# Three of four blocks of cross-attention exponentials and maxima moved one place ahead in a software pipeline of four engines

## The reference

```python
# cross-attention, 8 heads of 64, no mask
xn  = layernorm(x)
sim = einsum('bihd,bjhd->bhij', xn @ Wq, ctx @ Wk) / 8
x   = x + (softmax(sim) @ (ctx @ Wv)) @ Wo + bo
# attention whose projections are mixtures of 16 experts
h   = layernorm(x)
rw  = gating(h)                       # softmax over the active experts, [tokens, 16]
q, k, v = [einsum('bte,bted->btd', rw, einsum('btc,ecd->bted', h, w)) for w in (q_proj, k_proj, v_proj)]
attn  = softmax(causal(q @ k.T / 8)) @ v
mixed = attn[:, :, None, :] * rw[..., None]
x   = x + einsum('bted,edc->btc', mixed, o_proj)
```

## Time and profile before

| what | us |
|---|---|
| time, median of 3 runs | 2771.4 (2769.01 to 2772.56) |
| profiled execution, its own time | 2767.65 |
| its span, from the first to the last instruction | 2765.9 |
| TensorE busy (matmuls) | 2698.9 |
| VectorE busy | 2233.7 |
| ScalarE busy | 1226.8 |
| GpSimd busy | 1186.2 |

### The profile page before, as it was taken

One profiled execution on the slowest core, in us unless ns is written; L12 is line 12 of the kernel. 1 busy time (PEld: TensorE's weight loads), 2 busy tenths in 40 slices (PEclk: granted clock), 3 DMA queues, 4 the chain that ended last, 5 costly groups with the idle time before them and its releaser, 6 DMA issues.

```text
span 2765.9 us, 65910 instructions
## 1 busy us (share of the span) xinstructions
PE 2698.9 (98%) x19012; PEld 2582.4 (93%) x19012; DVE 2233.7 (81%) x6371; ACT 1226.8 (44%) x4240; POOL 1186.2 (43%) x1739
## 2 busy tenths in 40 slices
PE   5999999999999999999999999999999999999996
PEld 4999999999999999999999999999999999999996
DVE  6788888888888888888888878888888888888875
ACT  4444444444444444544444444444445444444441
POOL 1353443444444444534434434444445344344343
PEclk8999999999999999999999999999999999999998
DMA  4111111111111111111111111211111111111111
GB/s 105 29 46 43 33 44 35 41 44 28 44 48 28 44 44 32 44 44 32 44 39 37 44 28 44 48 28 44 45 32 44 44 32 44 42 34 44 33 39 39
DMA packets 131437, 113.59 MB, mean 41 GB/s; under 512 B 24720, under 2 KB 130640, under 8 KB 131408
## 3 DMA queue, kind: packets, MB, share of 16 engines
q1 hardware_dynamic: 131408, 113.23, 16.9%
HBM read 95.38 MB, written 17.83 MB: 41 GB/s over the span
## 4 chain that ended last, share of the span: by engine, by line
PE 90%; ACT 4%; DVE 2%; issue 2%; POOL 0%; DMA 0%; DVEq 0%; ACTq 0%; SPq 0%; POOLq 0%
PE bank_b L373 12%; PE bank_b L374 11%; PE bank_b L375 11%; PE bank_a L375 10%; PE bank_a L374 10%; PE bank_a L373 10%; PE bank_c L373 5%; PE bank_c L375 5%; PE bank_c L374 5%; PE bank_a L487 4%; PE bank_c L551 1%; PE bank_a L447 1%; PE bank_a L446 1%; PE bank_a L418 1%; DVE k_stack L1011 1%
## 5 line engine op out<-in xcount | busy, mean ns | idle before, releaser
L373 PE MATMUL bank_b<-wqkv_hi,x2T_lo 128*128 128x384 f32 (+1 forms) x2048 | 719.8, 351 | 0.0
L374 PE MATMUL bank_b<-wqkv_lo,x2T_hi 128*128 128x384 f32 (+1 forms) x2048 | 693.8, 339 | 0.0
L375 PE MATMUL bank_b<-wqkv_hi,x2T_hi 128*128 128x384 f32 (+1 forms) x2048 | 688.7, 336 | 0.0
L1000 DVE SCALAR_TENSOR_TENSOR acc<-bank_b,rw,acc 128x192 f32<-128x192 f32 x1792 | 641.1, 406 | 4.9 <-PE bank_b L375 2.4
L1256 POOL TENSOR_TENSOR mixs_lo<-mix,mixs_hi 128x512 fp32r<-128x512 f32 x256 | 380.5, 1517 | 156.4 <-ACT mixs_hi L777 156.4
L373 PEld LDWEIGHTS bank_b<-wqkv_hi,x2T_lo 128*128 128x128 f32 x2048 | 386.1, 189 | 17.6 <-DVE acc L1000 17.2
L374 PEld LDWEIGHTS bank_b<-wqkv_lo,x2T_hi 128*128 128x128 f32 x2048 | 386.2, 189 | 0.0
L375 PEld LDWEIGHTS bank_b<-wqkv_hi,x2T_hi 128*128 128x128 f32 x2048 | 385.2, 188 | 0.0
L1178 POOL TENSOR_TENSOR pow_out<-pow_in,expo 128x2 f32<-128x2 f32 (+1 forms) x128 | 111.7, 873 | 607.6 <-DVE pow_in L862 508.3
L723 ACT ACTIVATE probs<-bank_a,s_max 128x77 f32<-128x77 f32 x1024 | 316.5, 330 | 56.6 <-DVE s_max L931 56.6
L373 PE MATMUL bank_c<-wo_hi,mixs_lo 128*128 128x256 f32 x1024 | 293.8, 287 | 3.7 <-POOL mixs_lo L1256 3.7
(11 more groups left out here) (195 smaller groups left out, 6926.9 us busy)
## 6 DMA issues: line engine op xcount, KB each, us to landing
rw_all<-rw_dram SPq DMA_DIRECT2D x128, 512.0 KB, 5.9
xt<-in_x_dram SPq DMA_DIRECT2D x64, 256.0 KB, 2.7
out_dram<-mix SPq DMA_DIRECT2D x64, 256.0 KB, 2.2
ct<-in_ctx_dram SPq DMA_DIRECT2D x64, 57.8 KB
ct<-in_ctx_dram SPq DMA_DIRECT2D x64, 19.2 KB
mix<-in_L_ffn_o_proj_dram SPq DMA_DIRECT2D x2, 512.0 KB, 4.4
rw_dram<-rwT SPq DMA_DIRECT2D x64, 16.0 KB, 1.4
x_tiles<-in_L_xattn_Wq_dram SPq DMA_DIRECT2D x1, 512.0 KB, 6.8
```

The lines of the kernel that those rows point to most:

```text
L373: nc.tensor.matmul(dst, lhs[1], rhs[0], start=start, stop=False)
L374: nc.tensor.matmul(dst, lhs[0], rhs[1], start=False, stop=False)
L375: return nc.tensor.matmul(dst, lhs[0], rhs[0], start=False, stop=stop)
L1000: V.scalar_tensor_tensor(acc[:, t, k, :], src, rw[:, t, e:e + 1], acc[:, t, k, :], ALU.mult, ALU.add).then_inc(b_evac, 1)
```

## The change

On VectorE the maxima of blocks 1, 2 and 3 of batch i+1 move from the start of step i+1 to the end of step i: block 1 behind c_pT and ahead of b_qkv 0, block 2 behind b_qkv 0, block 3 behind c_mix 0. On ScalarE the exponentials of blocks 1, 2 and 3 move in the same way: block 1 ahead of the copy of the attention result (c_pv), block 2 behind it, block 3 behind the rounding c_mix 0. No instruction is added or removed; the lists of TensorE, GpSimd and SyncE stay as they are.

```diff
 # ScalarE
                 do(earlier, c_mix, 3)
-                do(now, a_exp, 1)
-                do(now, a_exp, 2)
-                do(now, a_exp, 3)
                 do(now, a_pT, 0)
...
                 do(ahead, a_exp, 0)
+                do(ahead, a_exp, 1)
                 do(before, c_pv)
+                do(ahead, a_exp, 2)
                 do(before, c_mix, 0)
+                do(ahead, a_exp, 3)
                 do(before, c_mix, 1)
                 do(before, c_mix, 2)
 # VectorE
-                do(now, a_s, 1)
                 do(before, b_qkv, 5)
                 do(now, a_psum, 0)
-                do(now, a_s, 2)
-                do(now, a_s, 3)
                 do(before, b_qkv, 6)
                 do(now, a_psum, 1)
...
                 do(ahead, a_s, 0)
                 do(now, b_wsum)
                 do(before, c_pT)
+                do(ahead, a_s, 1)
                 do(now, b_qkv, 0)
+                do(ahead, a_s, 2)
                 do(now, b_qkv, 1)
                 do(now, b_qkv, 2)
                 do(before, c_mix, 0)
+                do(ahead, a_s, 3)
                 do(before, c_mix, 1)
```

## The result

The changed kernel takes 2824.7 us in the median of 4 runs (2822.9 to 2826.1), the kernel before 2770.8 beside it: a ratio of 1.0194, 95% interval 1.0176 to 1.0212, 54 us slower. The forecast was 2827.

The account below looks back on a forecast made before the run. TensorE, 98% busy, bounds the kernel, and VectorE's chain to b_qkv 4 delays it one for one. Three maxima (1.17 us) less 0.26 give 0.91 us, times 62 is 56 us: 2827 as the median, range 2799 to 2850.

Parts of the forecast that it names:

- a delay of 0.91 us in each of 62 steps: VectorE's b_qkv 4: 1.17 us of added maxima less 0.26 us given back; 62 times 0.91 is 56 us.
- VectorE's chain: VectorE's unbroken work from the first block's maximum to b_qkv 4, which TensorE's b_qkv 7 awaits; three maxima add 1.17 us.
- the wait for L1000: TensorE's wait for VectorE's accumulation: to grow from 17.2 to some 70 us, on two products instead of one.
- The starts worked out for the new order: VectorE's computed times: mixing 0 at 1038.79, mixing 1 at 1039.78, mixing 2 at 1041.03, b_qkv 4 at 1042.10.
- The term given back: Mixing 2 on VectorE stands 0.26 us less, as GpSimd's first remainder starts later beside it.
- the hold goes both ways: VectorE's multiply and GpSimd's remainder block each other: delay 0.91 us; 0.78 if only VectorE were held up.
- ScalarE hides the copy: Attention result's copy, delayed some 0.8 us, ends near 1038.3, before mixing 0 at 1038.79: 0.5 us to spare.
- The feared tie at the first rounding: ScalarE's third exponentials end as mixing 0's rounding is due, 1039.50; held back over 0.8 us, 2799 would follow (10%).
- The wait at b_qkv 6: TensorE waits some 0.35 us for b_qkv 3, ending 1.17 us later on VectorE; contained in b_qkv 7's wait.
- The waits of VectorE for the exponentials: Waits at L937 at the step's start, 0.98 us in the step shown: to go, with nothing gained on TensorE.
- The first steps: Steps at the kernel's start: same work in the same order on ScalarE, counted at nothing.
- rival (b): Same delay of 0.1 to 0.5 us, remainder still first: 1.2 to 1.6 us a step, 2846 to 2870; 9%.

Follow-up runs that it names:

- the maxima alone: Changed kernel with the exponentials of blocks 1 to 3 back at the start of the next step, maxima left moved: 2824.7 us, ratio 1.0192.
- one maximum at the head: Kernel before with only block 1's maximum moved ahead of b_qkv 0 on VectorE: 2792.0 us, ratio 1.0078.
- mixing from PSUM: Changed kernel with mixing multiplies reading the attention result from PSUM instead of its SBUF copy, which is still made and waited for: 2797.1 us, ratio 1.0094.
- the changed kernel with the swap: Changed kernel with b_qkv 4 put ahead of mixing 2 on VectorE: 2822.7 us, ratio 1.0186.
- the kernel before with PSUM: Kernel before with the mixing multiplies reading the attention result from PSUM, the copy still made and waited for: 2754.6 us, ratio 0.9939.
- the swap in the kernel before: Kernel before with b_qkv 4 put ahead of mixing 2 on VectorE: 2765.3 us, ratio 0.9980.

## Why the prediction was right

The forecast was a delay of 0.91 us in each of 62 steps; the chain's delay is 0.87 and the step 0.88 us longer. By its steps:

- VectorE's chain ends last at b_qkv 7, and its delay passes to TensorE one for one. This is shown by the wait for L1000, by the maxima alone (same loss) and by one maximum at the head (0.40 us for 0.39).
- The starts worked out for the new order were within 0.04 us: mixing 0 at 1038.79 + 22.41 = 1061.20 (1061.19), the remainder at 1062.62 (1062.61), mixing 2 at 1063.44 (1063.43), b_qkv 4 at 1064.51 (1064.47).
- The term given back, 0.26 us, was 0.28 (mixing 2: 1.40 to 1.12). That the hold goes both ways, as the Trainium skill says ("SBUF — State Buffer", "Who interferes with whom"), is seen in the remainder's 1.39 us beside mixing 1; mixing from PSUM, which leaves mixing one SBUF input, ends it.
- ScalarE hides the copy: it runs from 1060.25 to 1060.68, its user starts at 1061.19, and with the exponentials back at their old place the loss is the same. The feared tie at the first rounding came out on time: 0.71 us behind mixing 0's start.
- The wait at b_qkv 6, put at 0.35 us, is the other 62 of the 124 waits; b_qkv 6 starts 0.36 us later in its step.
- The waits of VectorE for the exponentials went, and brought nothing, as TensorE waits for nothing at their place. VectorE's idle time only moved to the transposed probabilities. What VectorE waited for, in the kernel before and in the changed one:

```profile
DVE p_sum L937 <- ACT probs L723: 169.2, 127, 2.2
...
DVE pT_lo L898 <- ACT pT_hi L685: 11.3, 64, 0.3
```
```profile
DVE pT_lo L898 <- ACT pT_hi L685: 242.4, 66, 3.9
...
DVE p_sum L937 <- ACT probs L723: 2.1, 1, 2.1
```

- The first steps were put at nothing, and no loss from them is shown. Ahead of the loop the third and fourth maxima now precede the first reciprocal. Before and after:

```profile
35.49 0.19 DVE L937 RECIPROCAL p_sum<-p_sum 128x8 f32<-128x8 f32 x1
```
```profile
35.84 0.86 DVE L931 TENSOR_REDUCE s_max<-bank_a 128x4 f32<-128x308 f32 x2
36.61 0.19 DVE L937 RECIPROCAL p_sum<-p_sum 128x8 f32<-128x8 f32 x1
```

The reciprocal comes 1.12 us later, 0.77 of it by the two maxima. The second batch's first maximum is at 73.51 against 71.10. But it is at 70.90 in the changed kernel with the swap, which has the same maxima ahead, and at 72.60 in the kernel before with PSUM, which has none of them ahead. The mean granted clock of the first 74 us, in which both of its levels (1.2 and 2.4 GHz) occur, differs from one profiled execution to the next: 0.84 and 0.82 in the kernel before and the changed one, 0.86 and 0.79 in the other two. And 62 times 0.88 us is already the 54 us that were measured.

One slip had no consequence: the range was to end at the lower edge of rival (b), which is 2846 by its own figures, and was written as 2850.

## What to carry to other kernels

Where an engine is busy for 98%, look at the few waits that recur in every step, follow the waiting one back to its chain's head, and count what a change puts between the two; work that leaves idle time elsewhere gains nothing. A deadline list (which eviction must be done when the matrix engine comes back to its bank) says where moved work is free. After each repair look for the next chain that ends within half a microsecond: here VectorE's eviction and GpSimd's remainders stood that close, and mending the first alone gave nothing.

## What was not expected of the hardware

When VectorE's mixing multiply and GpSimd's remainder come to their places within 0.04 us of each other, hundredths of a microsecond decide which of the two stands. In the swap in the kernel before, a multiply with a recorded start 0.03 or 0.04 us behind the remainder's stands until that is through (1.81 us instead of 0.68). At 0.01 or 0.02 us behind, the multiply goes first, and the remainder takes 1.84 to 1.86 us instead of 1.30. The first kind of step is 0.29 us longer than the second, a loss of 0.16 us a step in the mean of the 59. Reading one input of the multiply from PSUM costs it nothing (0.68 us either way) and takes the hold away on both engines (the remainders take 1.28 to 1.31 us).
